# Rounded halves for two of six tokenizer records, and work moved between VectorE and ScalarE, in a one-core ViT kernel

## What is computed

```python
xb = 2.0 * jnp.pi * xyz[..., None] * freq_bands            # (4, 3, 512, 192, 6)
feat = jnp.concatenate([jnp.sin(xb), jnp.cos(xb)], axis=-1).reshape(b, n, -1)
h = jnp.einsum('bnf,of->bno', feat, W)                     # 6912 features to 192
h = concat([cls_tok, h])                                   # one class token ahead
# attention: normalize, q, k, v and forget gates, cumulative sums over tokens
h = numerator / denominator
mu, var = mean(h), var(h)
normed = (h - mu) / jnp.sqrt(var + 1e-05) * gamma + beta
h = h + normed @ Wo
# feed-forward on layernorm(h): a shared expert of 768 units, and the best two of eight routed ones
h = h + alpha * shared + (1.0 - alpha) * routed
```

## Time and profile before

| | us |
|---|---|
| median of 3 executions | 556.94 |
| lowest, highest | 554.76, 557.33 |
| the profiled execution | 554.62 |
| its span, first to last instruction | 552.8 |
| granted TensorE clock over the span | 1.000 |

### The profile page before, as it was taken

How to read it: one execution, slowest core, us unless ns; L and a number is a source line. 1 busy time by engine, 2 the same in 40 slices (tenths; PEclk the granted TensorE clock), 3 DMA queues, 4 the chain that set the end, 5 groups by cost and what they waited for, 6 DMA issues and landing times.

```text
span 552.8 us, 9034 instructions
## 1 busy us (share of the span) xinstructions
PE 535.8 (97%) x3235; PEld 504.8 (91%) x3235; DVE 370.3 (67%) x1065; ACT 244.4 (44%) x343; POOL 180.3 (33%) x205
## 2 busy tenths in 40 slices
PE   5999999999999999999999999999999999999997
PEld 5998999899999899999989999978877899999865
DVE  8637787534868637978853995468998256666437
ACT  3465464755324764243565422264142135555410
POOL 6413134122234311765212460002601414444510
PEclk9999999999999999999999999999999999999999
DMA  8900067000000001110000010510103441531174
GB/s 330 341 23 20 7 219 250 20 10 20 20 19 21 20 0 27 62 59 0 1 1 10 20 59 1 185 54 30 50 0 125 157 136 47 171 99 51 52 216 142
DMA packets 23488, 42.49 MB, mean 77 GB/s; under 512 B 2502, under 2 KB 15044, under 8 KB 23348
## 3 DMA queue, kind: packets, MB, share of 16 engines
q1 hardware_dynamic: 19560, 33.31, 18.4%
q0 software_dynamic: 3472, 8.07, 4.1%
q10 hardware_dynamic: 412, 0.53, 0.4%
HBM read 31.74 MB, written 14.79 MB: 84 GB/s over the span
## 4 chain that ended last, share of the span: by engine, by line
PE 80%; DVE 11%; ACT 4%; issue 2%; DMA 1%; ACTq 0%; DVEq 0%
PE ps L1369 44%; PE ps L1571 3%; PE ps L1624 2%; PE ps L1626 2%; PE ps L1533 1%; PE ps L1602 1%; PE ps L1603 1%; PE ps L1604 1%; PE ps L1606 1%; PE ps L1605 1%; DMA r<-r 1%; PE ps L1537 1%; PE ps L1535 1%; PE ps L1536 1%; PE ps L1534 1%
## 5 line engine op out<-in xcount | busy, mean ns | idle before, releaser
L1369 PE MATMUL ps<-w_tok,feat 128*128 128x192 f32 x1728 | 289.4, 328 | 7.5 <-ACT feat L502 6.2
L1369 PEld LDWEIGHTS ps<-w_tok,feat 128*128 128x128 f32 x1728 | 282.9, 191 | 8.7 <-issue 8.7
L426 POOL TENSOR_SCALAR feat<-fx 128x512 int32<-128x512 f32 x108 | 93.4, 880 | 189.4 <-PE ps L1369 185.8
L511 ACT ACTIVATE feat<-feat 128x1536 f32<-128x1536 f32 x35 | 52.0, 1485 | 110.1 <-DVE feat L805 110.1
L801 DVE SCALAR_TENSOR_TENSOR feat<-fx,feat 128x512 f32<-128x512 f32 x105 | 76.5, 781 | 1.8 <-POOL feat L426 1.5
L462 POOL DMA_INDIRECT ydram<-yr,xs x39 | 37.8, 969 | 53.9 <-DVE yr L1127 53.9
L514 ACT ACTIVATE feat<-feat,half_pi 128x1536 f32<-128x1536 f32 x35 | 54.6, 1561 | 0.0
L456 POOL DMA_INDIRECT slots<-pay_a,posi x17 | 17.4, 1025 | 75.2 <-DVE posi L1053 71.8
L805 DVE TENSOR_SCALAR feat<-feat 128x1536 int32<-128x1536 int32 x35 | 37.3, 1066 | 1.2
L1571 PE MATMUL ps<-w_down,hid_ring 128*128 128x192 f32 x192 | 35.4, 328 | 2.2 <-DVE H L1085 2.2
L616 ACT ACTIVATE s_ring<-ps 128x512 f32<-128x512 f32 x24 | 14.4, 599 | 52.4 <-PE ps L1537 52.4
(11 more groups left out here) (306 smaller groups left out, 859.6 us busy)
## 6 DMA issues: line engine op xcount, KB each, us to landing
slots<-in_blank SPq DMA_DIRECT2D x1, 5031.0 KB, 19.2
w_tok<-in_wT SPq DMA_DIRECT2D x7, 576.0 KB, 8.9
fx<-in_xT SPq DMA_DIRECT2D x15, 256.0 KB, 2.7
xs<-slots SPq DMA_DIRECT2D x5, 645.0 KB, 5.8
yin<-ydram SPq DMA_DIRECT2D x8, 384.0 KB, 6.6
raw_a<-in_wea SPq DMA_DIRECT2D x4, 384.0 KB, 5.4
raw_b<-in_web SPq DMA_DIRECT2D x4, 384.0 KB, 6.0
w_tok<-in_wT SPq DMA_DIRECT2D x4, 288.0 KB, 7.5
```

What stands on the lines that cost most here:

```text
L426: ins = pool.tensor_scalar(feat[:, k % SLOTS, i, :].bitcast(I32), x[:, x_block(k), :], f_col[:, fi:fi + 1], 1.0, ALU.mult, ALU.mult)
L511: act.activation(feat[:, k % SLOTS, 0:3, :], feat[:, k % SLOTS, 0:3, :], ACT.Sin, scale=TWO_PI).then_inc(sin_ready, 1)
L1369: ins = pe.matmul(ps[:, TOK[a % 2][t // 2], (t % 2) * D:(t % 2 + 1) * D], feat[:, k % SLOTS, i, t * P:(t + 1) * P], w_tok[:, k, i, :], sta ...
```

## The change

In groups 1 to 7 of images 1 to 3 (21 groups, never image 0), records 4 and 5 are no longer float32 products. The weights are split once, in image 0: `weight_high` (ScalarE, rounding copy to float32r) and `weight_low` (GpSimd, the rest). The features are split for each group: `feature_high` (ScalarE, 128x1024 copy) and `feature_low` (VectorE, 128x1024 subtraction). TensorE then makes, for each record and tile, one product of the high features with the low and the high weights side by side (384 columns) and one of the low features with the high weights (192 columns). Image sums now take one bank a tile, the same four banks for every image; `take_h` copies tile by tile, two pieces each for images 1 to 3, and VectorE adds the pieces before the norm. Groups 0 and 8 are multiplied tile by tile instead of record by record.

Besides: the absolute values move from VectorE to ScalarE (`ACT.Abs`, ahead of each sine, with a wait between); the heads aren't divided, since the norm takes it out if its epsilon is scaled by the squared denominator; the doubled 64 columns are copied by ScalarE (`twice`) and TensorE's `attn8` waits for that; in the last stage `places(4)` stands one to two steps later and `down(18)` after `tile_hidden_t(0)`; the scratch for GpSimd's DMA descriptors is 4096 bytes a partition instead of the default.

```diff
-TOK = ((0, 1), (2, 3))
+TOK = (0, 1, 2, 3)
@@ gpsimd
+            def weight_low(k):
+                w0 = w_at(k)
+                pool.wait_ge(whi_ready, k)
+                pool.wait_ge(tok_group, k + 1)
+                pool.tensor_tensor(w_r[:, w0 + 4:w0 + 6, :].rearrange("p i o -> p (i o)"),
...
+                                   ALU.subtract).then_inc(wlo_ready, 1)
@@ scalar, in sines
                     act.wait_ge(r_ready, q + 1)
+                    act.activation(feat[:, k % SLOTS, 3:6, :], feat[:, k % SLOTS, 0:3, :], ACT.Abs).then_inc(abs_ready, 1)
+                    act.wait_ge(abs_ready, q)
                     act.activation(feat[:, k % SLOTS, 0:3, :], feat[:, k % SLOTS, 0:3, :], ACT.Sin,
...
+            def feature_high(a, k):
...
+                act.wait_ge(sin_ready, 2 * (NG * a + k) + 2)
+                act.activation(f_hi[:, k % 2, :, :].rearrange("p i t -> p (i t)"),
+                               feat[:, k % SLOTS, 6 - R3:6, :].rearrange("p i t -> p (i t)"),
+                               ACT.Copy).then_inc(fhi_ready, 1)
...
+            def twice(a):
+                act.wait_ge(xn2_ready, a + 1)
+                act.activation(payload(a)[:, :, D:XD], payload(a)[:, :, P:D], ACT.Copy).then_inc(twice_ready, 1)
...
@@ scalar, the order in image 0
             sines(0, 7)
+            weight_high(5)
             attn8(0)
@@ scalar, the order in images 1 to 3
                 if b >= 2:
                     router(b - 1)
+                feature_high(b, 2)
                 sines(b, 3)
                 odds(b)
                 take_v(b, 0)
+                feature_high(b, 3)
                 sines(b, 4)
                 take_v(b, 1)
                 log_odds(b)
@@ vector, in remainders
-                ins.then_inc(r_raw, 1)
-                dve.wait_ge(r_raw, q + 3)
-                dve.tensor_scalar(feat[:, s, 3:6, :].bitcast(I32), feat[:, s, 0:3, :].bitcast(I32), 0x7FFFFFFF, None,
-                                  ALU.bitwise_and).then_inc(r_ready, 1)
+                ins.then_inc(r_ready, 1)
+                if a >= 1 and 2 <= k <= NG3 + 1:
+                    feature_low(a, k - 1)
@@ vector, attn0
+                    if a >= 2:
+                        dve.tensor_tensor(H[:, a - 1, :, :], H[:, a - 1, :, :], xn[:, :, :], ALU.add).then_inc(h_sum, 1)
+                        dve.wait_ge(h_sum, a - 1)
@@ vector, the last stage
                 if q == Q_RK:
                     router(B)
                     gates(B)
-                    places(B, [0])
...
                 hidden(q)
...
                 if q == Q_RK:
+                    places(B, [0])
+                if q == Q_RK + 2:
                     places(B, [1])
-                if q == Q_RK + 2:
                     places(B, [2])
@@ tensor
+            def record(a, k, i, t):
+                tokens = slice(t * P, (t + 1) * P)
+                out_ = ps[:, TOK[t], D:2 * D]
+                if halved(a, k, i):
+                    f = f_hi[:, k % 2, i - 6 + R3, tokens]
+                    pe.matmul(ps[:, TOK[t], 0:2 * D], f, w_r[:, w_at(k) + i:w_at(k) + i + R3 + 1:R3, :], start=False,
+                              stop=False, skip_group_check=True)
+                    return pe.matmul(out_, f_lo[:, k % SLOTS, i, tokens], w_r[:, w_at(k) + i + R3, :], start=False,
+                                     stop=False, skip_group_check=True)
...
+                if q >= 1 and k in (0, NG - 1):
+                    pe.wait_ge(sin_ready, 2 * q + 2)
+                    for t in range(NT):
+                        if k == 0 and t < NT - 1:
+                            pe.wait_ge(h_tile, (NT - 1) * (a - 1) + t + 1)
...
@@ tensor, in attn8
                     pe.transpose(ps[:, A2, i * P:(i + 1) * P], pay_[:, i, 0:P], ident)
+                pe.wait_ge(twice_ready, a + 1)
                 for i in range(nt):
                     ins = pe.transpose(ps[:, A1, i * P:(i + 1) * P], pay_[:, i, P:XD], ident)
@@ tensor, the routed tiles
-                if i == 1:
-                    down(NQB - 1)
                 if 2 <= i < NTILE + 2:
                     tile_hidden_t(i - 2)
+                if i == 2:
+                    down(NQB - 1)
```

More of the change, by code:

```diff
@@ L31 @@
 SLOTS = 3
+NG3 = NG - 2
+R3 = 2
 CLS = 2
@@ L467, in _ @@
                     rounds(b, k)
+                    if b == 0 and k > SLOTS:
+                        weight_low(k - SLOTS)
+                    if b == 1 and k < 2:
+                        weight_low(NG - SLOTS + k)
                     if b >= 2:
@@ L592, in attn8 @@
                 xh_a_, _, xh_b_, _ = operands(a)
+                if a < B:
+                    twice(a)
                 act.wait_ge(xpose3, a + 1)
@@ L665, in _ @@
             sines(0, 3)
+            weight_high(1)
             act.wait_ge(consts_ok, 2)
@@ L668, in _ @@
             sines(0, 4)
+            weight_high(2)
             sines(0, 5)
+            weight_high(3)
             attn6(0)
@@ L713, in _ @@
                     move_k(B)
+                if q == Q_X3:
+                    twice(B)
                 silu(q)
@@ L758, in _, with layernorm @@
         def _(dve):
-            def layernorm(src, dst, a, which, TP, nt, done, twice=False, parts=(0, 1, 2)):
+            def layernorm(src, dst, a, which, TP, nt, done, over=None, parts=(0, 1, 2)):
                 n0 = (3 * a + which) * LNS
@@ L770, in layernorm @@
                     for i in range(nt):
-                        ins = dve.bn_stats(st[0:TP, i, :], src[0:TP, i, 0:D])
+                        ins = dve.bn_stats(st[0:TP, i, :], src(i))
+                    if over is not None:
+                        for lo, d in over:
+                            n = d.shape[1]
+                            ins = dve.tensor_scalar(den[0:TP, lo:lo + n], d, DEN_EPS, None, ALU.add)
                     next_(ins)
@@ L774, in layernorm @@
                         ins = dve.bn_aggr(mv[0:TP, i, :], st[0:TP, i, :])
+                    if over is not None:
+                        ins = dve.scalar_tensor_tensor(den2[0:TP, 0:nt], den[0:TP, 0:nt], LN_EPS, den[0:TP, 0:nt],
+                                                       ALU.mult, ALU.mult)
                     next_(ins)
@@ L1355, in project @@
                     pe.wait_ge(wt_in[k], x_parts(k))
-                elif a >= 2 and k == 0:
-                    pe.wait_ge(h_ready, a - 1)
+                if q >= 1 and k in (0, NG - 1):
+                    pe.wait_ge(sin_ready, 2 * q + 2)
+                    for t in range(NT):
+                        if k == 0 and t < NT - 1:
+                            pe.wait_ge(h_tile, (NT - 1) * (a - 1) + t + 1)
+                        if k == 0 and t == NT - 1:
+                            pe.wait_ge(h_ready, a)
+                        for i in recs:
+                            ins = record(a, k, i, t)
+                        if k == NG - 1 and t < NT - 1:
+                            ins.then_inc(tok_tile, 1)
+                    ins.then_inc(tok_group, 1)
+                    return
                 for i in recs:
@@ L1546, in up_one @@
                     pe.wait_ge(silu_ready, q)
-                if q in (1, 2) and bank in TOK[1]:
+                if q == 0 and i == 0:
                     pe.wait_ge(h_ready, B)
```

134 lines of the change are left out of this document (81 added, 53 removed).

## The result

The changed kernel takes **563.85 us** (median of 6 executions, 562.34 to 566.64) against 557.11 before (6 executions). The ratio is 1.0139, 95% interval 1.0112 to 1.0167: 1.4% slower. The forecast of 556.0, and its range to 561.5, were wrong.

The account below looks back on a forecast made before the run. TensorE, busy 535.8 of 552.8 us, was taken as the bound. The terms -6.5 + 4.3 + 4.0 - 2.8 = -1.0 us gave 556.0 us on the median of 556.94, with an 8 in 10 range of 550.5 to 561.5.

Parts of the forecast that it names:

- The products: Tokenizer groups of images 1 to 3: a pair takes 286.6 ns, saving 38.4 ns on each of 168, 6.5 us.
- Rivals A and C: A: pairs at 262.5 ns, ScalarE not late, 549.5 us, chance 0.32; C: narrow product costs 162.5 ns, 562.5 us, chance 0.06.
- the prediction's second estimate: By the Trainium skill's rule a pair takes 269 ns, saving 9.4 us; not the figure used.
- Image 0: Waits for the sine of (0, 4) and at `attn8(0)` grow by 1.8 and 2.5 us: together +4.3 us.
- The k chain: Images 1 to 3, before `attn3`: third groups' saving lost (0.9 us), ScalarE late (3.1 us): +4.0 us.
- Rival B: ScalarE becomes the bound between the norm and the k chain, two us more an image: 562 us, chance 0.17.
- The last stage: VectorE's waits go, against 0.6 us of new wait for the tiles and 0.2 at batch 4's norm: -2.8 us.

Follow-up runs that it names:

- a_again: The changed kernel run once more, unedited: 564.44 us, ratio 1.0166 to the kernel before.
- a_places_before: The changed kernel with the positions of batch 4 written where they were before, `down(18)` still moved: 559.60 us, ratio 1.0083.
- a_scratch8192: The changed kernel with 8192 instead of 4096 bytes of descriptor space for the indirect DMAs: 561.52 us, ratio 1.0084.
- a_twice_early: The changed kernel with `twice(0)` ahead of `sines(0, 7)` and `weight_high(5)` behind `attn8(0)`: 563.62 us, ratio 1.0123.
- b_again: The kernel before run once more, unedited: 554.93 us, ratio 0.9983.
- a_f32_records: The changed kernel with all records in float32 again, no high and low parts, no second piece of H: 567.21 us, ratio 1.0211.
- b_scratch4096: The kernel before with 4096 bytes of descriptor space for the indirect DMAs: 557.21 us, ratio 0.9999.
- b_wait_short: The kernel before with one 128 x 512 copy in place on ScalarE ahead of the sine of (0, 4): 561.11 us, ratio 1.0089.

## Why the prediction was wrong, by its steps

**The products: right.** In the trace of the changed kernel pairs start 0.286 us apart, the forecast 286.6 ns:

```profile
140.13 0.36 PE L1445 MATMUL ps<-w_r,X 128*128 128x384 f32 x1
140.33 0.25 PE L1447 MATMUL ps<-w_r,f_lo 128*128 128x192 f32 x1
140.42 0.36 PE L1445 MATMUL ps<-w_r,X 128*128 128x384 f32 x1
```

Rivals A and C are out: neither 262.5 nor 337.5 ns, and not the 269 of the prediction's second estimate either. The sum is shown, its two terms are not: by these starts the wide product takes 0.20 and the narrow one 0.09, where I had 0.175 and 0.112. That the weight load bounds the narrow product fits the sum and was not tested by itself.

**Image 0: the mechanism right, the size 0.8 us short.** (0, 4) waits 2.94 (2.8 forecast), by the very steps named: absolute value, table load, sine. The chain at `attn8(0)` (start us, us, what):

```profile
66.73 0.58 DVE ya L875
...
67.33 0.64 DVE ya L876
...
69.64 2.00 DVE feat L903 x3
71.66 1.49 ACT feat L546
73.18 1.48 ACT feat L548
74.66 1.47 ACT feat L551
```

The steps behind the remainders are as forecast, and the wait is 3.44 (2.8). Two steps of the norm take 0.58 and 0.64 us where their like take 0.15 to 0.16; that is 0.9 us. GpSimd is busy just then (64.95 to 67.96) with a `weight_low`, 1.0 us, and the multiples that stand behind it. The other traces bear it out: in this one, `a_again`, `a_places_before`, `a_scratch8192` and `a_twice_early`, where the multiples run beside these steps, they take 0.57 to 0.58 and 0.63 to 0.64 us, and in the five other versions of the changed kernel, where GpSimd has ended just before, 0.15. Not every small step is slowed: the TENSOR_SCALAR steps at 66.20 to 66.70 take 0.14 in the same company. This term was not in the sum.

**The k chain: mechanism right, size somewhat over.** The three waits sum to 2.7 us (4.8 forecast, in the bounds of 2 to 8), but the stretch at 278.75 had put TensorE behind in image 3. In `a_again` and `a_places_before`, without that stretch, they sum to 3.7 and 3.8: +3.0 and +3.1 against +4.0. No wait for `f_lo` or H appeared. Rival B, ScalarE as the bound there, did not come.

**The last stage: wrong in sign, -2.8 forecast, +1.9 measured.** The gains came where forecast: no wait before L1580 (-0.6), L1605 (-0.8), and two of the three outputs' waits are gone (-1.1 and -0.5). These stand against them:

```profile
406.06 1.54 PE L1686 MATMUL ps<-w_down,hid_ring 128*128 128x192 f32 x8 [1.43 <-DVE H L1176]
418.76 0.24 PE L1620 MATMUL ps<-wra_hi,X 128*128 128x10 f32 x1 [0.57 <-issue]
...
452.86 0.45 PE L1698 MATMUL ps<-pack,xs 128*128 128x128 f32 x1 [3.06 <-DMA xs<-slots]
...
458.54 0.44 PE L1717 MATMUL ps<-e_hi,xhr 128*128 x1 [0.70 <-DVE xlr L1204]
```

The first output's wait grew from 0.61 to 1.43. The waits of 0.57 (the router's first product) and 0.70 (the second tile's products, ahead of which `down(18)` stood before) are new and were at nothing in the sum. The wait for the first tile is 3.06 us, 0.6 forecast. The positions end at 436.05, 13.75 us before TensorE would have asked for the tile (452.86 - 3.06), where before they had 18.3 (443.00 - 424.70). These 4.6 us less are what I had (3.3 later, and TensorE 1.1 earlier), of which 3.8 were to spare. What the sum lacked is the gap of 2.16 us more in the scatters, since I gave the smaller descriptor space no line at all: 4.6 + 2.2 - 3.8 = 3.0. `a_places_before`, without the lateness, has no wait; `a_scratch8192`, without the gap, has 1.5.

**The failed step, beside the last stage: a microsecond of waiting was priced at a microsecond.** The sum took TensorE's rate as a constant. Up to the last stage the waits and pairs alone came to +0.6 us in the profiled execution, where I had +1.8. The clock is the larger of the two misses, 8.5 us in the profiled execution and about 4.3 in the medians, against 4.7 for the last stage: three waits of about 3 us were made, each of which can be followed by a stretch at 1.2 GHz. The profile of before could have warned me: its longest wait inside the work was 1.1 us, and the forecast itself listed two of 2.8, a kind of wait that no row had a price for. It should have been bounded from both sides, as the unseen costs of the other engines were; above, by a slower TensorE for some stretch behind each wait. The Trainium skill (TensorE: Matmul & The Clock Gate, HAM oscillation — how this bites in real kernels) says as much: a wait can make the array fall back to half rate, and the loss is half of the time spent so. The traces agree (0.50 in every such stretch, 1.7 us lost in 3.41; 1.3 for each of two by the medians at 0.994 and 1.000), and go further: `b_again` has such stretches with no wait ahead of them.

How often does it happen? A single wait tells little: (0, 4) with 2.9 us of wait in `a_f32_records` had no stretch in the profiled execution, and had two in a row in `a_again`. The 16 profiled executions together say more. Of their 19 waits of 2.9 to 5.4 us inside the work, 17 have a stretch that begins before their end or less than 2 us behind it. The 7 waits of 1.1 us at (0, 4) have none, nor have those of 1.4, 2.0 and 2.1 us at `attn8(0)`; the one of 1.5 us at the first tile has. Of the 64 times that the router's twenty products run, 24 are followed within 1.4 us, or joined, by one. No stretch inside the work stands anywhere else, but for one at the wait of 6.1 us in `b_scratch4096`. What decides between yes and no at one place was not settled.

## What to carry to other kernels

Where TensorE has run without a break, a wait grown to 3 us or more can cost some 1 to 2.5 us beyond its length (1.9, 2.8 and 4.3 us of added wait cost 4.3, 5.0 and 5.6 here); keep waits near 1 us, or price the slow stretch behind them. Read the granted clock of every execution beside its time, since the one profiled may be at 1.000 when most are not. A change that relieves the bounding engine should first be freed of what it puts on the path: here the same products, with a few small pieces of work in another place, went from 1.4% slower to 0.65% faster.

## What the hardware showed that I had not expected

- Every stretch at 1.2 GHz inside the work lasted 3.41 us or twice that. 24 of the 43 went with twenty products of 10 columns in 2.2 us, most of them without idle time; in the kernel before, too.
- With 4096 bytes of descriptor space GpSimd stood idle for 2.41 to 3.06 us ahead of the fourth scatter of batch 4, in every such trace; with 8192 bytes or the default it was 0.30. Batch 3, with eight scatters as well, had no such gap.
- Two steps of VectorE on two rows took 0.57 and 0.63 us instead of 0.15 while GpSimd wrote its multiples.
- The table load of a sine costs nothing while ScalarE waits for its data, and 1.28 us as soon as another function of ScalarE on the same data stands ahead of it (`b_wait_short`: 1.9 us more wait by a copy of 0.63).
